# Two of a block's four normalised tiles on VectorE, as a product with a broadcast tensor

## The reference

```python
def _layernorm(x, axis=-1, eps=1e-05):
    m = jnp.mean(x, axis=axis, keepdims=True)
    v = jnp.var(x, axis=axis, keepdims=True)
    return (x - m) / jnp.sqrt(v + eps)

def _L0_attn_ref(x, W_off, b_off, W_attn, b_attn, W_out, b_out):
    off = (x @ W_off + b_off).reshape(Bx, Nx, H, P, 2)
    w = jax.nn.softmax((x @ W_attn + b_attn).reshape(Bx, Nx, H, P), axis=-1)
    idx = off[..., 0].astype(jnp.int32)          # wrapped and clipped to 0..127
    g = jnp.take_along_axis(x[:, 0, :], idx.reshape(Bx, -1), axis=1).reshape(Bx, Nx, H, P)
    s = jnp.sum(g * w, axis=(2, 3))
    return jnp.broadcast_to(s[..., None], (Bx, Nx, C)) @ W_out + b_out

def _L0_ffn_ref(x, ...):
    # 2 shared experts for each token, and the best 2 of 8 routed ones,
    # weighted by the softmax of their logits; an expert is
    # silu(x @ w1.T) * (x @ w3.T) @ w2.T, with a hidden size of 256
    ...

xn = _layernorm(x, axis=-1)
x = x + _L0_attn_ref(xn, ...) + _L0_ffn_ref(xn, ...)
```

## Time and profile before

| | |
|---|---|
| Median of three runs | 502.98 us (502.68 to 503.12) |
| The profiled execution | 503.18 us, its span 501.4 us |
| TensorE, matmuls busy | 432.6 us, 86% of the span |
| VectorE busy | 331.3 us, 66% |
| ScalarE busy | 229.1 us, 46% |
| GpSimd busy | 231.1 us, 46% |
| Product of VectorE (L894), 16 | 13.8 us in all, 329 ns at the shortest, 1279 at the longest |
| Subtraction of GpSimd (L775), 16 | 1112 ns at the shortest, 1232 at the longest |

### The profile page before, as it was taken

How to read it: one execution, slowest core, us unless ns; L and a number is a source line. 1 busy time by engine, 2 the same in 40 slices (tenths; PEclk the granted TensorE clock), 3 DMA queues, 4 the chain that set the end, 5 groups by cost and what they waited for, 6 DMA issues and landing times.

```text
span 501.4 us, 14718 instructions
## 1 busy us (share of the span) xinstructions
PE 432.6 (86%) x5200; PEld 376.1 (75%) x5200; DVE 331.3 (66%) x956; ACT 229.1 (46%) x432; POOL 231.1 (46%) x179
## 2 busy tenths in 40 slices
PE   0167676677899999999999999999999999999990
PEld 0156534354577777777788999999999999999990
DVE  3799799989768799999966776344434444344440
ACT  0588841163224544444443454444444444444440
POOL 0234400146754433333000000688888888887663
PEclk9999998999999999999998999999999999999995
DMA  8999400000331111111302432354444444432000
GB/s 238 284 171 174 74 1 1 5 32 18 99 112 34 54 44 55 48 43 48 96 2 96 140 110 95 75 59 64 63 55 66 55 60 60 60 37 23 4 2 1
DMA packets 50683, 34.58 MB, mean 69 GB/s; under 512 B 9408, under 2 KB 44224, under 8 KB 50624
## 3 DMA queue, kind: packets, MB, share of 16 engines
q1 hardware_dynamic: 32048, 23.88, 20.4%
q0 software_dynamic: 15296, 8.53, 12.4%
q10 hardware_dynamic: 3280, 1.36, 1.1%
HBM read 14.87 MB, written 20.69 MB: 71 GB/s over the span
## 4 chain that ended last, share of the span: by engine, by line
PE 72%; DVE 19%; issue 2%; ACT 2%; ACTq 2%; DMA 1%; POOL 1%; DVEq 0%; POOLq 0%
PE pY L616 17%; PE pY L466 9%; PE pAB L596 9%; PE pAB L598 8%; PE pAB L597 8%; PE pAB L451 4%; PE pAB L453 4%; PE pAB L452 4%; PE pV L491 3%; PE pV L478 3%; DVE units L894 3%; PE pV L579 2%; DVE hbuf L923 2%; DVE hot L834 2%; ACTq L630 2%
## 5 line engine op out<-in xcount | busy, mean ns | idle before, releaser
L798 POOL DMA_INDIRECT out_dram<-hot,rows x92 | 142.5, 1549 | 110.9 <-DVE hot L1173 86.0
L1167 DVE SCALAR_TENSOR_TENSOR hbuf<-pAB,units 128x512 f32<-128x512 f32 x92 | 63.6, 691 | 103.9 <-PE pAB L598 103.9
L596 PE MATMUL pAB<-xT,wsp 128*128 128x128 f16 x736 | 129.6, 220 | 1.1 <-ACT xT L737 0.6
L597 PE MATMUL pAB<-xT,wsp 128*128 128x128 f16 x736 | 129.7, 220 | 0.0
L598 PE MATMUL pAB<-xT,wsp 128*128 128x128 f16 x736 | 129.6, 220 | 0.0
L788 POOL DMA_INDIRECT sorted_rows<-rows,slot x64 | 69.4, 1084 | 112.2 <-DVE hbuf L923 64.4
L616 PE MATMUL pY<-wsp,hbuf 128*128 x736 | 103.0, 282 | 1.0 <-issue 0.7
L747 ACT ACTIVATE units<-pAB 128x512 f32<-128x512 f32 x92 | 55.0, 598 | 105.5 <-PE pAB L598 105.5
L616 PEld LDWEIGHTS pY<-wsp,hbuf 128*128 128x128 f32 x736 | 89.7, 192 | 1.7 <-issue 1.3
L701 ACT ACTIVATE units<-pAB 128x512 f32<-128x512 f32 x64 | 38.1, 597 | 113.8 <-PE pAB L453 113.8
L596 PEld LDWEIGHTS pAB<-xT,wsp 128*128 x736 | 72.5, 98 | 2.6 <-issue 2.1
(11 more groups left out here) (137 smaller groups left out, 558.0 us busy)
## 6 DMA issues: line engine op xcount, KB each, us to landing
sorted_rows<-c_pad_row SPq DMA_DIRECT2D x1, 6026.0 KB, 43.7
rows<-sorted_rows SPq DMA_DIRECT2D x46, 131.0 KB, 2.2
base<-in_x SPq DMA_DIRECT2D x4, 1024.0 KB, 8.2
out_dram<-base SPq DMA_DIRECT2D x16, 256.0 KB, 2.5
wraw<-in_wall SPq DMA_DIRECT2D x8, 256.0 KB
out_dram<-hot,rows POOLq DMA_INDIRECT x92, 3.3
sorted_rows<-rows,slot POOLq DMA_INDIRECT x64
wsp<-in_wall SPq DMA_DIRECT2D x8, 128.0 KB, 2.8
```

Of the source, the lines that this page charges most:

```text
L596: pe.matmul(o, hi, x(0), start=True, stop=False)
L597: pe.matmul(o, hi, x(1), start=False, stop=False)
L798: pool.indirect_dma_start(out_rows, bass.IndirectOffsetOnAxis(ap=xr[:, t // 2 % X_RING, t % 2, DEST:DEST + 1].bitcast(U32), axis=0), yt[:, ...
L1167: v.scalar_tensor_tensor(hbuf[:, r % 4, :], pAB[:, 2 * (r % 2) + 1, :], 1 / (XS * WS), silu[:, r % 2, :], ALU.mult, ALU.mult).then_inc(d_h ...
```

## The change

Of a block's four tiles ScalarE normalises two in place of three, and VectorE two in place of one. VectorE's instruction was TENSOR_SCALAR: one tensor and two values for each partition, subtract and then multiply. It is now SCALAR_TENSOR_TENSOR: the mean is still one value for each partition, and the factor is read as a second tensor, 128 x 128 elements broadcast from the column `st[:, 7, t]` in SBUF. The semaphore is raised by the second of the two instructions.

```diff
@@ normalise (ScalarE)
-                for j in range(TPB - 1):
+                for j in range(TPB // 2):
                     t = TPB * i + j
                     a = nc.scalar.activation(xs[:, r, j, :], base[:, t, :], ACT.Identity, bias=st[:, 1, t:t + 1],
                                              scale=st[:, 7, t:t + 1])
@@ VectorE
-            def normalise_fourth(g, r):
+            def normalise_half(g, r):
                 i = 4 * g + r
                 if i >= 4:
                     dve.wait_ge(rows_lo, i - 3)
-                t = TPB * i + TPB - 1
-                v.tensor_scalar(xs[:, r, TPB - 1, :], base[:, t, :], st[:, 0, t:t + 1], st[:, 7, t:t + 1],
-                                ALU.subtract, ALU.mult).then_inc(xs_fourth, 1)
+                for t in (TPB * i + TPB - 2, TPB * i + TPB - 1):
+                    done = v.scalar_tensor_tensor(xs[:, r, t % TPB, :], base[:, t, :], st[:, 0, t:t + 1], st[:, 7, t:t + 1].broadcast_to([P, P]),
+                                                  ALU.subtract, ALU.mult)
+                done.then_inc(xs_half, 1)
 
             def rows_high(g, r):
                 i = 4 * g + r
                 dve.wait_ge(xs_ready, i + 1)
-                dve.wait_ge(xs_fourth, i + 1)
+                dve.wait_ge(xs_half, i + 1)
...
-            pipeline(dve, NB, 4, 4, [(0, normalise_fourth), (0, later_parts), (0, rows_high), (0, shared_low), (4, read_projections)])
+            pipeline(dve, NB, 4, 4, [(0, normalise_half), (0, later_parts), (0, rows_high), (0, shared_low), (4, read_projections)])
```

More of the change, by code:

```diff
@@ L283, in layer_kernel @@
         xs_ready = sem("xs_ready")
-        xs_fourth = sem("xs_fourth")
+        xs_half = sem("xs_half")
         rows_hi = sem("rows_hi")
```

## The result

The changed kernel takes 508.57 us (median of four, 508.35 to 509.63) against 503.05: the ratio is 1.0114, with a 95% interval of 1.0097 to 1.0132. So it is slower by 5.5 us. The forecast was 510.7 in a range of 506.0 to 512.5; the sum of its terms, 7.7, was 2.2 too large.

A forecast was written before the change was run, and what follows sets the result against it. The prediction took the VectorE chain up to block 15's cast, in steady running a GpSimd-VectorE loop, as the bound. Terms 1.0 + 2.4 + 1.1 + 3.2 gave +7.7 us, so 510.7, range 506.0 to 512.5.

The forecast's parts named there:

- The bound and the pass-through: VectorE carries the chain of waits up to block 15's cast; a shift there reaches the kernel's end whole.
- The value of nothing for ScalarE's tile: In steady running ScalarE is already 0.58 us ahead, so taking one of its three tiles a block gains nothing.
- That the new form is held by GpSimd: VectorE's product with two SBUF tensors waits for GpSimd's subtraction like the old form, ending 0.14 us behind it.
- Blocks 0 to 2: The second products delay the first three blocks by 0.9 to 1.1 us, taken as 1.0.
- the cheaper of the two ways given: Block 1's second product beats the subtraction, and block 2's work is done at 25.38, not 25.63 if it loses.
- Blocks 3 and 4: The second product waits for the whole subtraction, delaying the statistics: +1.18 us each, 2.4 in all.
- a lead of 0.07 lost the contest above, so no lead loses it: In blocks 3 and 4 the second product, starting level with GpSimd's subtraction at +0.60, must wait until it ends.
- the rival in which the pair keeps GpSimd out: VectorE issues both products before GpSimd gets in: 0.26 us each in blocks 3 and 4, 507 to 508 total; chance 16%.
- Block 5: The first product wins, the second waits for the subtraction's end, and the statistics start later: +1.1 us.
- Blocks 6 to 15: The first product is held, the second follows it and delays the next instruction: +0.32 us a block, 3.2 in all.
- the first product wins in steady running: Variant inside the forecast: subtraction put off 0.13 us, second product held, +0.19 a block, 509.4 total; 69% together with forecast.

The follow-up runs named there:

- form_alone: The kernel before with only its one VectorE product a block written as SCALAR_TENSOR_TENSOR with the broadcast factor, ScalarE keeping three tiles: 502.45 us, ratio 0.999.
- factor_psum: The changed kernel with the scales copied to a free PSUM bank and the broadcast factor read from there: 502.68 us, ratio 0.9986 to the kernel before.
- low_memset: The changed kernel with GpSimd's subtraction replaced by a memset of zeros, which reads nothing, and its block loop written out: 501.17 us, measured once.
- count_alone: The changed kernel with both VectorE products in the old form, TENSOR_SCALAR: 510.19 us, ratio 1.0136 to the kernel before.
- pair_ahead: The changed kernel with the read of the projections moved behind the next block's two products, so these start earlier: 504.93 us, ratio 1.0036 to the kernel before.

## Why the prediction was right in direction and too large

*The bound and the pass-through* held: 5.58 at the last cast, 5.5 in the span. *The value of nothing for ScalarE's tile* held in the changed kernel, where no cast waits for it; `form_alone` shows that with three tiles ScalarE becomes the bound as soon as VectorE's product is free.

*That the new form is held by GpSimd* held, and `factor_psum` and `low_memset` show which two reads meet. (The prediction says that the trace of before has no row of the new form beside GpSimd's arithmetic; L827, which it uses in the paragraph before, is one.)

*Blocks 0 to 2*: 1.0 forecast, 0.74 measured. Block 1's second product, 0.09 ahead, won its contest, the cheaper of the two ways given:

```profile
21.54 0.61 DVE L894 SCALAR_TENSOR_TENSOR units<-base,hot 128x128 f32<-128x128 f32 x2
21.90 1.23 POOL L775 TENSOR_TENSOR rows<-units,rows 128x512 f16<-128x512 f32 x1 [8.39 <-DVE rows L902]
```

For that way the prediction has +0.88 (25.38 against 24.50). The other 0.14 is no saving of the change: in this trace the statistics already start at 16.48, where they started at 16.62. Without it the way given comes out to 0.01.

*Blocks 3 and 4*: 2.4 forecast, 1.46 measured: block 3 is 1.19 against 1.18, block 4 is 0.27 against 1.18. The step that failed is "a lead of 0.07 lost the contest above, so no lead loses it". The lead was read from the old form and carried to the new one. With the old form both steps are lost (`count_alone`); with the new one block 4 is won. Its cost (0.27) and its subtraction (1.33) are those of the rival in which the pair keeps GpSimd out (0.26, 1.3 or more); in block 3, in block 5 and from block 6 on that rival did not come true.

*Block 5*: 1.1 forecast, 1.14 measured.

*Blocks 6 to 15*: 3.2 forecast, 2.24 measured. Blocks 7 and 8, where L827 stands before the products and the subtraction starts first, have +0.34 and +0.32, the forecast's 0.32. The other eight have +0.19 to +0.20. That is the variant that the prediction counted out as "the first product wins in steady running" with +0.19 a block, and did not choose. The same failed step: which engine wins at a lead of 0.07 depends on the form of the instruction.

So the errors are the outcomes of contests decided by less than 0.1 us: 0.9 of the 2.2 us lies in block 4, 1.0 in the eight blocks, and of the 0.3 in the first three 0.14 is the earlier start. The mechanism and the prices of a won and of a lost contest were right (0.26 against 0.27, 0.19 against 0.19 to 0.20, 1.18 against 1.19, 0.32 against 0.32 and 0.34). Who would win was not known from the rows: the measured kernel is a mixture of the forecast, its variant and, in one block, a rival, and that all of them lay inside the range is the range's merit and not the sum's.

## What to carry to other kernels

Before moving work to VectorE beside a GpSimd instruction that reads SBUF, count its SBUF tensor operands: a broadcast is one too. The count is not the whole rule: TENSOR_SCALAR and the cast to f16 read one tensor here and were held as well. With one operand of the product in PSUM, or a lead of a few tenths of a microsecond over GpSimd, the same work was nearly free here; without either, each added instruction cost its time, and one in a group the rest of GpSimd's instruction. And when a stage ends sooner, look at what else was still running there: here a background transfer and TensorE's clock took the gain back.

## What the runs showed of the hardware that was not expected

The form decides a close contest. At a lead of 0.07 us TENSOR_SCALAR was held (1.27, and GpSimd 1.12), SCALAR_TENSOR_TENSOR was not (0.34, and GpSimd 1.26). TENSOR_SCALAR won from a lead of 0.10 on (`count_alone`, blocks 1 and 5, GpSimd 1.22 and 1.21). At equal starts the new form lost in step 3 and won in step 4, in two kernels alike (the changed one and `pair_ahead`); what tells these apart below 0.01 us stays open.

TensorE's clock can take back what an earlier stage gave. `factor_psum` begins the routing 1.67 us sooner than before (60.74 against 62.41), and its span ends 0.7 sooner. The windows of its profile (stretch, length, busy us and count of TensorE, weight loads, VectorE, ScalarE, GpSimd, granted clock, DMA share, GB/s):

```profile
75.00:80.00 5.00, 0.94 (x3) 0.39 (x4) 4.79 (x9) 0.00 (x0) 0.00 (x0) 0.76 0.00 0
...
90.00:95.00 5.00, 2.77 (x8) 1.31 (x9) 4.86 (x9) 0.00 (x0) 0.00 (x0) 0.63 0.00 0
95.00:100.00 5.00, 5.00 (x25) 3.28 (x25) 4.09 (x10) 1.19 (x2) 3.12 (x3) 0.69 0.08 27
```

The same windows of the kernel before:

```profile
75.00:80.00 5.00, 1.54 (x12) 1.15 (x9) 4.83 (x9) 0.60 (x1) 0.00 (x0) 1.00 0.00 0
...
90.00:95.00 5.00, 1.41 (x8) 0.78 (x8) 4.90 (x8) 0.00 (x0) 0.00 (x0) 1.00 0.00 0
95.00:100.00 5.00, 4.05 (x27) 2.55 (x26) 4.89 (x8) 1.20 (x2) 2.03 (x2) 1.00 0.04 13
```

TensorE is idle for some microseconds in both while VectorE works on the routing. In both the clock fell around 80 us (0.56 and 0.67 from 80 to 85), in `factor_psum` sooner. There it also fell from full to half between 91 and 98 us, so that matmuls of the shared experts were 0.43 apart and not 0.22, in a stretch that VectorE waited for; in the kernel before it stayed full there. Of the 1.79 us by which VectorE was earlier at the last cast, 0.57 are left at 99.5 us.

The clock differs between executions of one kernel too. Of the 21 of the kernel before beside `factor_psum`, the eight with a mean granted clock of 0.983 to 0.986 took 502.62 to 503.17 us, the five with 0.959 or 0.963 503.72 to 504.09. The three of `factor_psum` with 0.983 to 0.986 took 501.54 to 501.87. So at the same mean clock it gains 1.3 us (501.59 against 502.89), where the medians of all differ by 0.35. A stage's gain of one or two microseconds is within what this takes or gives.
